# A vision block with two layers of experts: a fourth score buffer, the projection in another bank, two slots of statistics, and matmuls whose result nobody reads

## The reference

```python
x = x + attention(ln_c(x))       # 64 dilated windows of 64 tokens, 16 heads of 8, 2-D rotary q and k
t = t + moe0(ln_t(t))            # 8 experts of 128 -> 256 -> 128, the best 2 of 8 per token
x = x + whiten(ln_c(x)) * gamma + beta
t = t + moe1(ln_t(t))            # 8 experts with an inner gated layer, best 2 of 8

def whiten(x):                   # x as 128 channels by N = 4096 tokens
    f = x - mean(x)
    cov = per 32 channels: f f' / (N - 1), mixed with EPS * eye
    sig = cov / trace
    P = eye
    for _ in range(3):
        P = (3 P - P P P sig) / 2
    return (P / sqrt(trace)) f
```

## Time and profile before

| what | us |
|---|---|
| median of 3 runs | 1042.8 |
| the profiled execution | 1043.76 |
| its span, first to last instruction | 1042.0 |
| PE busy in the span | 663.7 |
| DVE busy | 447.4 |
| POOL busy | 411.4 |
| ACT busy | 351.8 |
| mean granted clock | 0.738 |

### The profile page before, as it was taken

One profiled execution on the slowest core, in us unless ns is written; L12 is line 12 of the kernel. 1 busy time (PEld: TensorE's weight loads), 2 busy tenths in 40 slices (PEclk: granted clock), 3 DMA queues, 4 the chain that ended last, 5 costly groups with the idle time before them and its releaser, 6 DMA issues. The chain is left out here.

```text
span 1042.0 us, 16474 instructions
## 1 busy us (share of the span) xinstructions
PE 663.7 (64%) x5276; PEld 478.8 (46%) x5276; DVE 447.4 (43%) x1258; ACT 351.8 (34%) x861; POOL 411.4 (39%) x409
## 2 busy tenths in 40 slices
PE   3566756767665747564888883669127685668770
PEld 1233433535443535443655563557115564456650
DVE  1455564564547545331333334633503525223444
ACT  1343444234332424322444452413103232223440
POOL 2252343335424533565333332101571254653441
PEclk9557887575757576676899996665555766879995
DMA  6000089995000002222333304000024210424417
GB/s 242 21 10 3 11 131 170 168 166 88 11 6 11 21 20 51 54 59 57 97 100 100 99 25 149 21 0 1 31 65 81 52 34 31 104 63 110 89 35 243
DMA packets 81203, 73.72 MB, mean 71 GB/s; under 512 B 9263, under 2 KB 70840, under 8 KB 80736
## 3 DMA queue, kind: packets, MB, share of 16 engines
q1 hardware_dynamic: 71792, 54.51, 25.2%
q0 software_dynamic: 8896, 17.47, 5.1%
q10 hardware_dynamic: 432, 0.68, 0.2%
HBM read 35.37 MB, written 38.16 MB: 71 GB/s over the span
## 5 line engine op out<-in xcount | busy, mean ns | idle before, releaser
L592 POOL DMA_INDIRECT results<-work,rowbuf x142 | 138.1, 973 | 221.8 <-DVE work L906 94.7
L899 DVE SCALAR_TENSOR_TENSOR work<-work,rowbuf,bank 128x256 f32<-128x256 f32 x142 | 68.1, 480 | 215.6 <-ACT work L725 179.3
L1254 PE MATMUL bank<-Wh,xl 128*128 x142 | 80.2, 565 | 82.8 <-DVE xl L893 36.5
L1269 PE MATMUL bank<-W,work 128*128 x568 | 107.7, 320 | 34.3 <-ACT work L730 19.7
L1269 PEld LDWEIGHTS bank<-W,work 128*128 128x128 f32 x568 | 97.0, 224 | 67.9 <-issue 57.8
L725 ACT ACTIVATE work<-bank 128x256 f32<-128x256 f32 x142 | 54.6, 384 | 159.8 <-PE bank L1256 102.0
L1166 PE MATMUL bank<-Kbd,Q 32*64 32x256 f32 x512 | 62.3, 570 | 57.0 <-DVE Sx L852 45.1
L571 POOL TENSOR_TENSOR Sx<-Sx,srec 128x1024 f32<-128x1024 f32 x32 | 60.8, 1900 | 94.0 <-DVE srec L862 94.0
L1188 PE MATMUL bank<-PT,Vm 64*32 64x64 f32 x2048 | 46.7, 251 | 63.6 <-ACT PT L690 29.0
L1254 PEld LDWEIGHTS bank<-Wh,xl 128*128 128x128 f32 x142 | 31.3, 220 | 105.9 <-issue 105.6
L607 POOL DMA_INDIRECT region<-rows_a,where x64 | 63.1, 986 | 29.4 <-issue 26.0
(11 more groups left out here) (220 smaller groups left out, 1273.5 us busy)
## 6 DMA issues: line engine op xcount, KB each, us to landing
region<-pad SPq DMA_DIRECT2D x16, 1040.0 KB
rowbuf<-region SPq DMA_DIRECT2D x142, 65.0 KB
fetched<-results SPq DMA_DIRECT2D x16, 512.0 KB, 4.5
spare<-w1gv_dram SPq DMA_DIRECT2D x8, 640.0 KB
spare<-b_dram SPq DMA_DIRECT2D x71, 64.0 KB
results<-work,rowbuf POOLq DMA_INDIRECT x142
work<-w_dram SPq DMA_DIRECT2D x8, 256.0 KB, 2.9
W<-w_dram SPq DMA_DIRECT2D x2, 1024.0 KB, 12.6
```

Of the source, the lines that this page charges most:

```text
L592: pool.indirect_dma_start(results[layer], bass.IndirectOffsetOnAxis(ap=at, axis=0), ysb[:, T % YRING, :], None, bounds_check=PAIRS - 1, oo ...
L899: v.scalar_tensor_tensor(out=hh[:, i % 2, :], in0=sg[:, i % 2, :], scalar=rowbuf[:, i % RING, GATE_AT:GATE_AT + 1], in1=bank[:, b, FF:2 * FF],
L1254: mm(bank[:, b, :], low, wh, start=True, stop=False)
L1269: last = mm(bank[:, b, 0:P], hT[:, i % 2, ft * P:(ft + 1) * P], W2[layer][:, bass.ds(experts[i] * FT + ft, 1), :].rearrange("p a n -> p (a ...
```

## The change

Five edits.

1. `Sx` gets a fourth buffer, which lies in the second half of `spare`. `sub` of piece i waits for `PT` of piece i - 4.
2. `J` moves from bank 2 to bank 3.
3. In `ORDER`, `Vm0` and `Vm1` move from behind `ht` to the second place, and `J_add` moves from behind `K` to between `max` and `sub`.
4. `mv`, `var`, `rstd` and `nmr` get two slots, used in turn; the waits in `pool_power` and `dve_norm` look one block further back.
5. A helper `warm(b, n)` issues n matmuls on PE: bf16, 128x128 weights (`before_b`), 384 columns (`half`), into bank b. Nothing reads their result; what comes behind them overwrites it. It is called after the bank is claimed and before the wait for the data.

| called before | count x calls |
|---|---|
| the transposes `PT` of a piece | 8 x 32 |
| `white` | 6 x 8 |
| `turn`, in layer 1 only | 6 x 8 |
| `yturn` | 6 x 8 |
| `cov` | 6 x 8 |
| seven waits of the Newton chain | 3, 9, 6, 3, 6, 3, 6 |

```diff
+WARM_PIECE, WARM_BLOCK, WARM_CHAIN = 8, 6, 3
...
-ORDER = ("up", "J", "O", "S", "V0", "V1", "dn", "out", "xt", "ht", "Vm0", "Vm1", "T",
-         "a_y", "Kb0", "Kb1", "rows", "route", "white", "max", "sub", "sum", "Q", "K", "J_add", "exp", "Q0", "Q1", "norm",
+ORDER = ("up", "Vm0", "Vm1", "J", "O", "S", "V0", "V1", "dn", "out", "xt", "ht", "T",
+         "a_y", "Kb0", "Kb1", "rows", "route", "white", "max", "J_add", "sub", "sum", "Q", "K", "exp", "Q0", "Q1", "norm",
...
-BANK = {"T": 3, "V0": 3, "V1": 3, "turn": 3, "O": 2, "J": 2, "logits": 2, "place": 2, "xt": 1, "ht": 5, "dn": 4, "fold": 6}
+BANK = {"T": 3, "V0": 3, "V1": 3, "turn": 3, "O": 2, "J": 3, "logits": 2, "place": 2, "xt": 1, "ht": 5, "dn": 4, "fold": 6}
...
-        mv = {n: sb(f"mv_{n}", [P, BT, 2]) for n in "amc"}
-        var, rstd, nmr = ({n: sb(f"{w}_{n}", [P, BT]) for n in "amc"} for w in ("var", "rstd", "nmr"))
+        mv = {n: sb(f"mv_{n}", [P, 2, BT, 2]) for n in "amc"}
+        var, rstd, nmr = ({n: sb(f"{w}_{n}", [P, 2, BT]) for n in "amc"} for w in ("var", "rstd", "nmr"))
...
+        def sx(p):
+
+            k = p % BT
+            return Sx[:, k, :] if k < 3 else spare[:, UNIT * ROW:UNIT * ROW + HEADS * WIN]
...
-            after(pool, y_sb[s], BT * i)
-            pool.tensor_tensor(rstd[s][:, :], var[s][:, :], con("minus_half"), ALU.pow).then_inc(rstd_sb[s], 1)
+            after(pool, y_sb[s], BT * (i - 1))
+            pool.tensor_tensor(rstd[s][:, i % 2, :], var[s][:, i % 2, :], con("minus_half"), ALU.pow).then_inc(rstd_sb[s], 1)
...
-            after(dve, rstd_sb[s], i)
+            after(dve, rstd_sb[s], i - 1)
...
-                if i >= 3:
-                    wait_full(dve, "PT", i - 3)
-                v.tensor_tensor(Sx[:, i % 3, :].rearrange("p (h m) -> p h m", h=HEADS),
+                if i >= BT:
+                    wait_full(dve, "PT", i - BT)
+                v.tensor_tensor(sx(i).rearrange("p (h m) -> p h m", h=HEADS),
...
+        def warm(b, n):
+
+            for _ in range(n):
+                nc.tensor.matmul(bank[:, b, 0:3 * P], before_b, half[:, :].bitcast(BF16), start=True, stop=True)
...
                 b = pe_claim(name, i)
+                warm(b, WARM_PIECE)
                 pe.wait_ge(p_nrm, i + 1)
...
+                if i >= BLOCKS:
+                    warm(b, WARM_BLOCK)
                 pe.wait_ge(y_sb["m"], BT * (i + 1))
...
                 b = pe_claim("cov", i)
+                warm(b, WARM_BLOCK)
                 wait_freed(pe, "mean", i)
...
+            warm(5, 3 * WARM_CHAIN)
             pe.wait_ge(newton, TRACE_STEP - 1)
...
+                warm(5, 2 * WARM_CHAIN)
                 pe.wait_ge(newton, FIRST_STEP + 4 * it)
```

More of the change, by code:

```diff
@@ L569, in pool_step @@
                 pool.wait_ge(p_rec, i + 1)
-                p = Sx[:, i % 3, :].rearrange("p (h m) -> p h m", h=HEADS)
+                p = sx(i).rearrange("p (h m) -> p h m", h=HEADS)
                 pool.tensor_tensor(p, p, srec[:, i % BT, :].unsqueeze(2).to_broadcast([P, HEADS, WIN]), ALU.mult)\
@@ L662, in act_step @@
                 for k in range(BT):
-                    act.activation(ya[:, k, :], X[:, i * BT + k, :], ACT.Identity, bias=nmr["a"][:, k:k + 1],
-                                   scale=rstd["a"][:, k:k + 1]).then_inc(y_sb["a"], 1)
+                    act.activation(ya[:, k, :], X[:, i * BT + k, :], ACT.Identity, bias=nmr["a"][:, i % 2, k:k + 1],
+                                   scale=rstd["a"][:, i % 2, k:k + 1]).then_inc(y_sb["a"], 1)
             if name == "T":
@@ L686, in act_step @@
                 wait_freed(act, "S", i)
-                act.activation(Sx[:, i % 3, :], Sx[:, i % 3, :], ACT.Exp).then_inc(p_exp, 1)
+                act.activation(sx(i), sx(i), ACT.Exp).then_inc(p_exp, 1)
             if name == "PT":
@@ L703, in act_step @@
                     act.activation(rows[:, at + k, 0, 0:P], X[:, (i % BLOCKS) * BT + k, :], ACT.Identity,
-                                   bias=nmr["m"][:, k:k + 1], scale=rstd["m"][:, k:k + 1]).then_inc(y_sb["m"], 1)
+                                   bias=nmr["m"][:, i % 2, k:k + 1], scale=rstd["m"][:, i % 2, k:k + 1]).then_inc(y_sb["m"], 1)
                 act.wait_ge(y_sb["m"], BT * (i + 1))
@@ L741, in act_step @@
                 for k in range(BT):
-                    act.activation(yc[:, i % 2, k, :], X[:, i * BT + k, :], ACT.Identity, bias=nmr["c"][:, k:k + 1],
-                                   scale=rstd["c"][:, k:k + 1]).then_inc(y_sb["c"], 1)
+                    act.activation(yc[:, i % 2, k, :], X[:, i * BT + k, :], ACT.Identity, bias=nmr["c"][:, i % 2, k:k + 1],
+                                   scale=rstd["c"][:, i % 2, k:k + 1]).then_inc(y_sb["c"], 1)
             if name == "yturn":
@@ L793, in dve_norm @@
                 dve.wait_ge(st[s], i * BT + k + 1)
-                v.bn_aggr(mv[s][:, k, :], stats[s][:, k, :]).then_inc(mv_sb[s], 1)
+                v.bn_aggr(mv[s][:, i % 2, k, :], stats[s][:, k, :]).then_inc(mv_sb[s], 1)
             dve.wait_ge(mv_sb[s], BT * (i + 1))
-            after(dve, rstd_sb[s], i)
-            v.tensor_scalar(var[s][:, :], mv[s][:, :, 1], eps_, None, ALU.add).then_inc(var_sb[s], 1)
+            after(dve, rstd_sb[s], i - 1)
+            v.tensor_scalar(var[s][:, i % 2, :], mv[s][:, i % 2, :, 1], eps_, None, ALU.add).then_inc(var_sb[s], 1)
         def dve_shift(s, i):
@@ L802, in dve_shift @@
             dve.wait_ge(rstd_sb[s], i + 1)
-            nc.vector.scalar_tensor_tensor(out=nmr[s][:, :], in0=mv[s][:, :, 0], scalar=-1.0, in1=rstd[s][:, :],
+            nc.vector.scalar_tensor_tensor(out=nmr[s][:, i % 2, :], in0=mv[s][:, i % 2, :, 0], scalar=-1.0, in1=rstd[s][:, i % 2, :],
                                            op0=ALU.mult, op1=ALU.mult).then_inc(nmr_sb[s], 1)
@@ L857, in dve_step @@
                 dve.wait_ge(p_exp, i + 1)
-                v.tensor_reduce(ssum[:, i % BT, :], Sx[:, i % 3, :].rearrange("p (h m) -> p h m", h=HEADS), AXIS_X, ALU.add)\
+                v.tensor_reduce(ssum[:, i % BT, :], sx(i).rearrange("p (h m) -> p h m", h=HEADS), AXIS_X, ALU.add)\
                     .then_inc(p_sum, 1)
@@ L1174, in pe_step @@
                     last = nc.tensor.transpose(bank[:, b + a // 4, (a % 4) * P:(a % 4 + 1) * P],
-                                               Sx[:, i % 3, a * P:(a + 1) * P], ident)
+                                               sx(i)[:, a * P:(a + 1) * P], ident)
                 last.then_inc(fill_done(name, i), 1)
@@ L1322, in _ @@
                 .then_inc(newton_ps, 1)
+            warm(5, WARM_CHAIN)
             pe.wait_ge(newton, 2)
             mm(bank[:, NEWTON1, 0:P], means[0:BLOCKS, :], means[0:BLOCKS, :], start=True, stop=True).then_inc(newton_ps, 1)
+            warm(5, 3 * WARM_CHAIN)
             pe.wait_ge(newton, TRACE_STEP - 1)
```

## The result

The changed kernel takes 1051.85 us, the median of 20 runs (1047.64 to 1058.29), against 1046.81 for the kernel before, measured beside it. The ratio is 1.0056, with a 95% interval of 1.0036 to 1.0076: 0.6% slower, where 1011 and "faster" were forecast. The time lies in the range; the direction is wrong.

A forecast was written before the change was run, and what follows sets the result against it. Attention was taken as bound by a chain between in-order queues, with PE often at the slow clock. Attention -26, covariance -1, Newton -1, whitening head -5, layer 1 tiles +1 sum to -32: 1011 us, range 975 to 1055.

The forecast's parts named there:

- -26 for attention: Attention, all eight blocks: the whole change saves 26 us, with bounds of +26 and about -60.
- bound of 12 for the bank: Attention's slow bound: moving J to bank 3 takes 12 off a loss of 38 us, leaving +26.
- the ordinary block's -3.2: Attention, after the second PT: its group is hidden, the clock holds, and S, V and Q run 3.2 us shorter.
- the route blocks -7.5 each: Two attention blocks with a route: 3 us from the bank, about 4 to 5 from warm work, 7.5 saved each.
- That DVE time ... ends in neither: Fourth score buffer: the DVE wait it removes, at most 17.8 us, shortens neither K chain nor J_add; 0, at best -5.
- the worst case I kept: Whitening head: the clock stays slow despite the groups of six, which then cost up to 13.5 us; -5 was taken.
- A: Rival, chance 0.17: unread matmuls run at the slow clock before ready transposes and the clock does not hold; slower, about 1073.
- B: Rival, chance 0.13: the clock stays up through attention, each of eight blocks some 4 us shorter again; about 980.
- C: Rival, chance 0.20: gain and price cancel, PE's gain ending in the DVE and POOL chain before S; 1033 to 1053.
- D: Rival inside the forecast, no own chance: data-flow edits do nothing, bank change gives only its late cases; 5 us more.
- the clock in 340 to 364 under 0.6: Sign of a wrong forecast: PE's granted clock still under 0.6 between 340 and 364 us.
- Sub late enough that PT waits for its bank: Sign of a wrong forecast, in attention: `sub` delayed so far that the transposes PT wait for their bank.

The follow-up runs named there:

- put held: Changed kernel with POOL waiting, before the put of a piece in attention, until ACT has copied O of that step; 1039.55 us, ratio 0.9953.
- kernel of streams: Separate kernel, computing nothing of the reference: PE streams alone, then beside POOL's indirect DMAs, some also beside POOL additions or plain DMAs; O's kind 191 matmuls in 2.88 us alone.

## Why the prediction was wrong

The versions form a chain of single steps from the kernel before to the changed one. The measured column is the difference of two ratios in us; each has an error of 4 to 6. What a step is worth depends on what stands already (J_add 14 or 0, the eight 6 or 20), so the column holds for this order of steps.

| step | ratio | measured | forecast |
|---|---|---|---|
| slots | 1 to 1.0014 | +1 | 0 |
| fourth buffer | to 0.993 | -9 | 0, at best -5 |
| unread, covariance to layer 1 | to 0.9822 | -11 (-4 in the new order) | -6 |
| eight before each PT | to 0.9882 | +6 | -14 |
| bank 3, early copy of V | to 0.9917 | +4 | -12 |
| J_add ahead of `sub` | to 1.0056 | +14 | 0 |

Forecast and result lie 38 us apart. Three steps of the sum failed, all in attention: the gain of the eight (20 of the 38), the bank change (16), and J_add, put at nothing (14); the buffer and the matmuls from covariance on gave 14 back. (The forecast's -26 for attention is split here by its own bound of 12 for the bank; its single terms for that add to 10.5.) J_add comes first below, since without the eight it costs nothing and with it the eight cost 20.

**J_add, put at nothing.** The sentence is: "who waits is PT's bank, after O, S and T on PE, 3 us later, so I cost it at nothing; without that cover it is the 2 us by which sub is later". In the block of the timeline `sub` starts 10.0 us after the scores do for 5.4 before, so it is later by 4.6 and not by 2, and DVE waits 31.7 us in 7 waits. I looked only at who needs the bank, and not at the rest of the chain behind `sub`: exp, sum, `norm`, and on POOL everything queued behind `norm`. The sum of that edit was made on PE and DVE. In block 8 its cost, 8 us of some 19 in the traces, is paid over POOL's queue, as a collision with work that no dependency ties to it. The rest is paid in the blocks before, and there the runs do not show the path: the chain behind `sub` is my reading. The two pairs of runs that isolate the edit say 14 us with the eight before PT, and 0 without them (0.986 and 0.9862).

**Eight before each PT.** The price per matmul was right: groups are 2.5 us start to start cold and 1.3 warm, 0.32 and 0.16 each, for 0.32 and 0.18. The Trainium skill, "TensorE: Matmul & The Clock Gate", Part 1 ("Wait — 56ns, not 53.3ns?"), has bf16 matmuls start N over 1.2 GHz apart cold and N over 2.4 GHz plus 2.5 ns warm; an estimate from that for 384 columns is 320 and 162 ns, and the 0.32 and 0.16 us of this trace agree. The forecast's division by PT was right in kind: the second group is the one that pays (7 to 10 us, where the ordinary block's -3.2 was met with -2.9 and -3.0 in the first two), and the other three cost 13 in eight blocks, 1.6 each, for a forecast of 2.7 (2.6 less 0.5, and 0.6). What was wrong is the gain, which I spread over all blocks: the forecast gave the route blocks -7.5 each, and they are shorter by 2.1 and 1.7 in the changed kernel. In the timeline of one of them the list fills DVE from 321.2 to 328.9 and PE waits 5.8 us for the `sub` behind it; that warm work on PE ends in this wait is my reading, no run isolates it.

**Bank 3.** J starts 1.6 after PT, as forecast, and O no longer waits for J_add. But J itself waits 11.6 us for V's copy in 7 waits, for a forecast of 1.65 each, which the sum set against the wait for J_add. The late J_adds were to bring 3 each beyond that, and nothing was won; that they lay in steps whose end was set elsewhere is my reading.

**Fourth buffer.** "That DVE time ... ends in neither" was wrong: the wait of DVE is gone and 9 us with it. In the traces at hand the gain is in the sixth and seventh block (49.2, 49.6 before; 47.5, 46.8 with the buffer) and the end of attention (28.1 and 25.1 to the last `max`).

**Covariance, Newton, whitening head.** The sizes were right in the changed kernel's trace: -1.2, -0.6 and -7.0. In Newton (12.2 us in all 14 traces with the groups, 12.5 to 12.7 without) the mechanism was right too. In covariance the hit is luck. The four traces with the two slots and no unread matmul in that loop take 40.3 to 41.6 us for it, those with them 41.6 to 42.6, and the kernel before 43.7: the groups gave nothing there, and what was gained came without them. A round at a granted 1.00 is 4.3 us without the groups and 5.3 with them, the forecast's +1.1; one at 0.50 without them was 6.4. Whether the slots, put at 0, or the state of the clock at the loop's start made these traces faster is open. In the head 28.9 us became 21.9 in ten traces, but the worst case I kept did come in part in four others: 23.5 us in two and 26.5 in two, with PE busy without a gap, entered at 1.00, and 0.50 granted in the middle of the same products and groups. From the trace with put held:

```profile
694.41:697.60 3.19, 3.19 (x17) 2.25 (x16) 0.00 (x0) 0.00 (x0) 0.00 (x0) 1.00 0.00 0
697.60:707.50 9.90, 9.90 (x34) 6.53 (x34) 4.18 (x21) 2.28 (x5) 1.55 (x2) 0.53 0.01 2
```

As a whole, three pairs of versions that differ in these matmuls alone put them at 3, 4 and 11 us, for a forecast of 6.

**The rivals.** A, the only one that forecast "slower", had the outcome and not the mechanism: the clock in attention rose to 0.77, and of its signs only the cold price of the first group is there. The 0.50 in the head came in four other traces alone. B's clock, up through all of attention, did not come. C's 1033 to 1053 hold the measured time, and its mechanism is in part seen: the groups of six cost what they give in covariance, though not in the head, and PE's wait for `sub` is still 31.0 us for 45.1. D fell twice over, the buffer won 9 and J_add lost 14. None of the rivals held POOL's queue. That the time lies in the stated range says little, for the range reached up to 1055 for A. Of the signs I named, "the clock in 340 to 364 under 0.6" was badly chosen: it is 0.90 after, but 0.83 with the buffer alone and no unread matmul, since other work has moved into that window. "Sub late enough that PT waits for its bank" was the right place and the wrong victim. One reading of the earlier trace rows was wrong as well: of the first 19 slices six hold a clock of 5, not most; the sum goes by the 0.68 of the earlier trace rows, which is right.

What stays open is by which path the late J_add costs 7 to 10 us in blocks 5 to 7, and why the tiles of layer 1 differ by up to 12 us between traces.

## What to carry to other kernels

When an operation is moved in an in-order queue, follow what is behind it through every engine to the end of the chain, and list what else stands in those engines' queues: here, in one block, a wait on DVE moved DMAs on POOL, and these slowed PE. Unread matmuls to hold the clock pay where PE waits anyway and warm work follows at once, one place in a block here, and are a plain cost elsewhere; try them place by place, and each part of a bundle alone, since here a bundle that loses 6 us holds one that wins 25. A stage that lands on its forecast is not yet understood: compare it with the version that lacks the edit, as covariance shows. Where a queue issues indirect DMAs, keep dense streams of small matmuls out of their time.

## What the runs showed of the hardware

While POOL issues indirect DMAs, streams of many short matmuls are starved: O's kind gets five or six matmuls per 0.75 us where it does 64 in 1.0 alone (from O to its copy it is 2.4 to 3.9 us for 1.1 under two such DMAs and 8 to 9.5 under five or six), scores take 4.44 for 2.41, and in the kernel of streams transposes and 384-column matmuls are unchanged beside four DMAs. Even alone a stream of O's kind stops after 191 matmuls for 1.15 us, with "issue" as its releaser. That PE's supply of instructions is near its limit there, and that POOL's DMAs share that supply, would explain both, and was not tested.

The same whitening products ran at either level of the clock. Without groups PE is fully busy with them at 0.50. Entered at 1.00 and with groups of six among them they stayed at 1.00 to the end in ten traces, and in four the clock fell to 0.50 in their midst, for 3 to 10 us, and rose again, with no gap in PE's work. Whether the entry or the groups do more to hold it was not separated.
